# Down projection and mixing of x: each 512-column matmul written as two of 256 columns

## The reference, cut to what matters

```python
x = fwht(x * SU_ug) / SCALE                              # mixing of x, 512 features
x_up = x @ W_up.T * (Wscale_ug[:INTER] * SCALE)          # 512 -> 2048
x_gate = x @ W_gate.T * (Wscale_ug[INTER:] * SCALE)
x = jax.nn.silu(x_gate) * x_up
x = fwht(x * SU_dp) / SCALE
x = x @ W_down.T * (Wscale_dp * SCALE)                   # 2048 -> 512, the down projection
# then: layernorm(x_in + x)
```

## Time and profile before

| | |
|---|---|
| median of 3 runs | 1555.98 us (1555.35 to 1555.99) |
| span of the profiled execution | 1556.1 us |
| TensorE (PE) busy | 1522.9 us, 98% of the span, 10152 matmuls |
| weight loads (PEld) | 10152, one for each matmul |
| VectorE, ScalarE, GpSimd busy | 67%, 40%, 30% |
| DMA, share of 16 engines | some 56% over the span |

### The profile page before, as it was taken

One profiled execution on the slowest core, in us unless ns is written; L12 is line 12 of the kernel. 1 busy time (PEld: TensorE's weight loads), 2 busy tenths in 40 slices (PEclk: granted clock), 3 DMA queues, 4 the chain that ended last, 5 costly groups with the idle time before them and its releaser, 6 DMA issues.

```text
span 1556.1 us, 26452 instructions
## 1 busy us (share of the span) xinstructions
PE 1522.9 (98%) x10152; PEld 1365.6 (88%) x10152; DVE 1035.8 (67%) x1790; ACT 625.6 (40%) x1289; POOL 466.1 (30%) x580
## 2 busy tenths in 40 slices
PE   6999999999999999999999999999999999999998
PEld 5977978888887888899999999999999999999997
DVE  6876786687678986864575576475566457557545
ACT  4163255236227665533333333333343334333322
POOL 5465456447438434500300130030030031003001
PEclk9999999999999999999999999999999999999999
DMA  7031122122122796677668668677767867766862
GB/s 283 1 108 76 35 82 102 35 82 102 64 77 93 286 380 256 245 263 282 231 243 290 236 211 292 226 243 255 269 225 236 292 216 255 277 231 220 282 225 95
DMA packets 92060, 307.44 MB, mean 198 GB/s; under 512 B 9888, under 2 KB 10272, under 8 KB 90144
## 3 DMA queue, kind: packets, MB, share of 16 engines
q1 hardware_dynamic: 90928, 301.54, 54.9%
q10 hardware_dynamic: 1008, 4.20, 0.7%
HBM read 255.37 MB, written 50.33 MB: 196 GB/s over the span
## 4 chain that ended last, share of the span: by engine, by line
PE 63%; DVE 5%; ACT 1%; issue 1%; POOL 1%; POOLq 0%; DVEq 0%; ACTq 0%
PE ff_bank_b L2058 16%; PE ff_bank_a L2058 11%; PE ff_bank_c L2058 11%; PE ff_acc L2085 7%; PE ff_acc L2086 7%; PE ff_acc L2078 7%; DVE ff_d_lo L1775 2%; PE ff_x_ps L2009 1%; PE ff_x_ps L2029 1%; ACT at_union L601 1%; DVE ff_h_lo L1794 1%; DVE ff_c L1826 0%; PE ff_x_ps L2017 0%; PE ff_x_ps L2018 0%; DVE ff_ring L1770 0%
## 5 line engine op out<-in xcount | busy, mean ns | idle before, releaser
L2058 PE MATMUL ff_bank_b<-ff_x_hi,ff_ring 128*128 128x256 f32 x1536 | 302.2, 280 | 2.5 <-DVE ff_c L1826 1.9
L2058 PEld LDWEIGHTS ff_bank_b<-ff_x_hi,ff_ring 128*128 128x128 f32 x1536 | 247.8, 188 | 3.8 <-issue 3.7
L2058 PE MATMUL ff_bank_b<-ff_x_lo,ff_ring 128*128 128x256 f32 x768 | 214.2, 279 | 0.0
L2058 PE MATMUL ff_bank_c<-ff_x_hi,ff_ring 128*128 128x256 f32 x1024 | 203.9, 282 | 0.0
L2058 PE MATMUL ff_bank_a<-ff_x_hi,ff_ring 128*128 128x256 f32 x1024 | 203.4, 282 | 0.0
L2085 PE MATMUL ff_acc<-ff_d_lo,ff_h_hi 128*128 128x512 f32 x504 | 198.0, 393 | 1.3 <-DVE ff_d_lo L1775 1.3
L2086 PE MATMUL ff_acc<-ff_d_hi,ff_h_lo 128*128 128x512 f32 x504 | 196.1, 389 | 0.0
L2058 PEld LDWEIGHTS ff_bank_a<-ff_x_hi,ff_ring 128*128 128x128 f32 x1024 | 165.3, 188 | 2.7 <-issue 0.2
L2058 PEld LDWEIGHTS ff_bank_c<-ff_x_hi,ff_ring 128*128 128x128 f32 x1024 | 165.1, 188 | 2.3 <-issue 2.3
L1822 DVE TENSOR_TENSOR ff_c<-ff_bank_b,ff_c 128x512 f32<-128x512 f32 x64 | 44.3, 692 | 175.3 <-PE ff_bank_b L2058 174.0
L2058 PEld LDWEIGHTS ff_bank_b<-ff_x_lo,ff_ring 128*128 128x128 f32 x768 | 143.7, 187 | 0.0
(11 more groups left out here) (323 smaller groups left out, 3471.2 us busy)
## 6 DMA issues: line engine op xcount, KB each, us to landing
ff_ring<-gu_scratch SPq DMA_DIRECT2D x392, 512.0 KB, 4.9
gu_scratch<-ff_ring SPq DMA_DIRECT2D x56, 512.0 KB, 4.4
at_xt<-in_xt SPq DMA_DIRECT2D x4, 2048.0 KB, 8.4
at_xn<-in_x SPq DMA_DIRECT2D x32, 256.0 KB, 2.9
x_scratch<-at_x SPq DMA_DIRECT2D x32, 256.0 KB, 2.0
ff_raw<-in_wgu SPq DMA_DIRECT2D x8, 1024.0 KB, 7.8
at_wd_a<-in_wd SPq DMA_DIRECT2D x8, 512.0 KB, 4.7
mixed_scratch<-at_wd_a SPq DMA_DIRECT2D x8, 512.0 KB, 3.2
```

Source lines behind the costliest of these rows:

```text
L2058: i = pe.matmul(bank[:, m, :], r[:, a, m, c, :], b[:, k, c, :], start=(k < 3 and m == 0 and c == 0 and b is x_hi and a == 0), stop=(m == 1 ...
```

## The change

Every matmul of 512 columns in `mix_x`, `last_down` and `down` becomes two of 256 columns, the left half of the moving operand and of the output first and then the right half, with the same weights. No tile moves in memory, and no wait and no signal is added or taken away. `start` stands on the first half of a bank's first product only, since it clears the marks of the whole bank; the halves of one bank make one group, with the check of groups skipped. `mix_down` and the first block's `mix_first` keep their 512 columns.

```diff
@@ mix_x
-                pe.matmul(x_ps[:, :], hr[:, :], xs_hi[:, :], start=True, stop=False)
-                pe.matmul(x_ps[:, :], hr[:, :], xs_lo[:, :], start=False, stop=True).then_inc(xh_ps.sem, 1)
+                for b in (xs_hi, xs_lo):
+                    for n in range(2):
+                        half = slice(HB2 * n, HB2 * n + HB2)
+                        i = pe.matmul(x_ps[:, half], hr[:, :], b[:, half], start=b is xs_hi and n == 0, stop=b is xs_lo and n == 1, skip_group_check=True)
+                i.then_inc(xh_ps.sem, 1)
@@ last_down
-                        i = three_passes(pe, acc[:, t, :], h_hi[q][:, j, k], h_lo[q][:, j, k], end_hi[:, j, :], end_lo[:, j, :], False, j == 1)
+                        for n in range(2):
+                            half = slice(HB2 * n, HB2 * n + HB2)
+                            for a, b in ((h_hi, end_hi), (h_hi, end_lo), (h_lo, end_hi)):
+                                i = pe.matmul(acc[:, t, half], a[q][:, j, k], b[:, j, half], start=False, stop=j == 1 and n == 1 and a is h_lo, skip_group_check=True)
@@ down
-                        pe.matmul(acc[:, t, :], h_hi[q][:, j, k], d_hi[:, j, :], start=first and j == 0, stop=False)
+                        for n in range(2):
+                            half = slice(HB2 * n, HB2 * n + HB2)
+                            pe.matmul(acc[:, t, half], h_hi[q][:, j, k], d_hi[:, j, half], start=first and j == 0 and n == 0, stop=False, skip_group_check=True)
...
-                        pe.matmul(acc[:, t, :], h_hi[q][:, j, k], d_lo[:, j, :], start=False, stop=False)
-                        i = pe.matmul(acc[:, t, :], h_lo[q][:, j, k], d_hi[:, j, :], start=False, stop=last and j == 1)
+                        for n in range(2):
+                            half = slice(HB2 * n, HB2 * n + HB2)
+                            pe.matmul(acc[:, t, half], h_hi[q][:, j, k], d_lo[:, j, half], start=False, stop=False, skip_group_check=True)
+                        for n in range(2):
+                            half = slice(HB2 * n, HB2 * n + HB2)
+                            i = pe.matmul(acc[:, t, half], h_lo[q][:, j, k], d_hi[:, j, half], start=False, stop=last and j == 1 and n == 1, skip_group_check=True)
```

## The result

The changed kernel takes 1571.92 us (1571.04 to 1575.14, 4 runs) where the kernel before takes 1555.76 (1555.35 to 1555.99, 4 runs): a ratio of 1.0105, with a 95% interval of 1.0091 to 1.0119. That is 1% slower, and 4 us above the top of the range. The profiled execution has a span of 1570.8 us (before: 1556.1).

What follows compares the result with a forecast made beforehand. TensorE, running without a gap, was taken to bound the kernel: 1556.1 + 11.1 + 0.2 + 0.2 - 0.7 = 1566.9, then - 6 - 1.9 + 1 for the products' rhythm gave 1560 us, range 1549 to 1568.

Steps and rivals of the forecast that it cites:

- What bounds the kernel: Token part: TensorE runs a steady step of 15.37 us without a gap, so added work is paid in full.
- The down pass: 24 matmuls become 48 at 0.1178 us each: 5.65 us in place of 5.48, +11.1 us over 63 passes.
- slow rhythm: Products' 256-column matmuls start 0.1178 us apart nearly always, against 0.1133 in the fast case.
- dearer than the slow rhythm: Rival: alternating halves in one bank with doubled loads cost more; above 1566 us, chance 0.08 shared with no long stretch fast.
- The rhythm of the products: Products and down passes: a fast or slow start now lasts to the next turn or wait, saving 4.5 ns per fast matmul.
- The gain of 6 + 1.9 us, less 1: Two of six long stretches fast, -6 us; short ones one in four, -1.9; some of today's fast stretches lost, +1.
- last_down and mixes: last_down's 24 matmuls become 48, at most +0.2 us; 28 mixes go from two to four, nothing to +0.3 in all.
- The one in step 7: Steady blocks, last step: product k = 5 waits for VectorE's ff_c; a longer down pass neither helps nor hurts.
- The -0.7 in the first block: First block: VectorE is slower at some six places, so part of the added pass time is waited out, at most 1.2 us.
- Cheap halves: Rival: down passes run fast by themselves, products behind start slow as now; 1554 to 1560 us, chance 0.14.
- the load left out: Rival: a pair's second half keeps the weights without a new load; 1554 to 1560 us, within a shared chance of 0.14.
- Long stretches fast: Rival: four or more of six long runs behind the waits start fast, -12 to -20 us; 1545 to 1553, chance 0.12.

Runs made afterwards that it cites:

- the probe: Kernel with the layer's work left out, streaming 256-column matmuls from tiles at several offsets in five patterns: 120.0 ns at 0, 117.8 or 113.3 at 16 and 48.
- the second probe: Like the probe, but with 512 columns or halves on a tile at 0 ahead of the products: products at 16 take 117.8 ns, at 48 113.3 or 117.8.

## Why the prediction was wrong, point by point

**What bounds the kernel: right.** TensorE without a gap, and all it does more is paid.

**The down pass: the first step that failed.** "If these go on in the slow rhythm of the products ahead of them": the price was read from the products, whose moving operand lies at 16, and given to a pass whose operand lies at 0. The text said that nothing in work or operands differs between the two rhythms. That holds for the two rhythms of the products, but it does not carry over to another tile. With the measured 0.1200 the pass is 5.76 and not 5.65, and 63 passes are +17.6 and not +11.1: 6.5 us. The right mechanism stood there as the rival "dearer than the slow rhythm" with "a price above the slow rhythm's would come on top of that". It had the wrong cause (bank and loads; the halves in another order and the probe refute it), shared a chance of 0.08 and had no price. The run with x at 0, where the same products cost 0.120, and the one with d at 16, where the slow passes cost 0.1178 a half, show what it is: the place. Why the place counts no run shows.

**The rhythm of the products: the second step that failed.** "After the change nothing of 512 columns is left behind the first block, so what a turn or a wait starts lasts to the next turn or wait." A down pass of halves at place 0 ends a fast stretch as well as one of 512 columns does, and no long stretch was fast. The gain of 6 + 1.9 us, less 1, did not come: 6.9 us. With d at 16 it did, with four of six long stretches fast where the prediction had two; how many is a draw that no run explains. The near cause is thus the same as in the step before: the place of d.

**last_down and mixes: too small.** Taken at +0.2 and +0.2; `last_down` costs 0.3 and the 28 mixes 0.5 (13.4 us against 12.9), with 0.48 us for four [the chain behind the turn, above] against 0.46 to 0.47 for two.

**Waits.** The one in step 7 was said to be untouched: it vanished, -1.9 us, as VectorE's two ff_d_lo beside GpSimd got shorter by 0.3 us a block (L1775 is 79.2 us before and 77.3 after, for 106). The -0.7 in the first block did not show: its 7 passes add 7 x 0.28 = 2.0 us, and the block is 2.1 longer; TensorE's waits there are 4.3 us where they were 3.9.

**The sum as it is now**: 1556.1 + 17.6 for the passes + 0.3 + 0.5 - 1.9 - 0.2 (34 fast products fewer) - 2.0 (the part ahead, by chance) = 1570.4; measured 1570.8. The two failed steps are 13.4 us; without the luck of the last term and of the vanished wait the miss would have been 4 us larger.

**The rivals.** Cheap halves and the load left out: refuted by 5.76 us a pass and by the 11744 loads. Long stretches fast: not here, but with d at 16 and at 48 they are most of what is gained. The page's 2.5 ns for each matmul (the Trainium skill, "TensorE: Matmul & The Clock Gate", "Back-to-back issue gap"), which that section gives for an isolated matmul, would have added 4.0 us; no run here shows such a cost: on one tile two halves take 240.0 ns against 226.7 for a whole one at place 0, 233.3 against 233.3 at 8, and in the fast rhythm 226.7 against 228.9 at 16.

## What to carry to other kernels

A price read from one loop holds for another only if the operands lie alike: compare the addresses of the tiles that are streamed, not only shapes and engines, and look for odd spare tiles such as a gap of 16 elements, since they may mark what a layout was tuned for. Before splitting or merging matmuls, measure the new width on the tile that it will read, since the best place for 512 columns was among the worst for 256; a shift of 64 bytes was worth 22 us here, more than the change itself. Where a kernel has two rhythms that are handed on, compare many runs and count the stretches: one long stretch is worth 2.9 us, and one kernel's runs lay over 22 us.

## What the runs showed of the hardware

- At a granted clock of 1.00 (2.4 GHz) 512 columns of these operands take 226.7 ns in the kernels with d at 0 and 228.9 with d at 16, and 256 columns 113.3, 117.8 or 120.0 at places 0, 16 and 48, by the place of the moving operand against a grid of 64 elements (256 bytes), in which the weights of all these kernels lay at 0. Whether the operand's own place counts or its distance from the weights was not tried.
- At places 16 and 48 two rhythms exist that last for hundreds of matmuls, through changes of line, bank and tile, until a transpose, a wait or another place comes between. At 8, 32 and 40 the second probe has two prices as well, 1 to 1.4 ns apart. At place 0 there is one, as dear as any, and it is the same from any start.
- With all operands at 48 the runs of one kernel lie at 1542 to 1564 us; the one traced, of 1564, has all its long stretches slow.
- A shift of one operand made the kernel before faster by 0.6% (1548.65 us); with halves and both operands at 48 it is 1548.83, at 16 1549.97. Which of the three is best these runs don't tell.
